# Weight loads and stores of the preparation issued from GpSimd's queue instead of SyncE's, in a scan layer beside a ternary feed-forward layer

## The reference, cut to what matters

```python
# x: (8, 4096, 1024) float32, one sequence of 4096 tokens for each core
xn = layernorm(x)
g = xn @ Wg + bg;  v = xn @ Wv + bv;  d = xn @ Wd + bd          # 1024 x 1024 each
h = linear_scan(sigmoid(g) * tanh(v), 0.001 + 0.998 * sigmoid(d))  # along the tokens

def weight_quant(w):      # ternary: each weight becomes -1, 0 or 1, times one scale
    scale = 1 / clip(mean(abs(w)), 1e-5)
    return clip(round(w * scale), -1, 1) / scale
def act_quant(x):         # 8 bits, one scale for each token
    scale = 127 / clip(max(abs(x), axis=-1), 1e-5)
    return clip(round(x * scale), -128, 127) / scale
gate = silu(act_quant(xn) @ weight_quant(w_gate).T)             # 4096 x 1024 weights
up   = act_quant(xn) @ weight_quant(w_up).T
f    = act_quant(gate * up) @ weight_quant(w_down).T            # 1024 x 4096 weights
out  = x + h + f
```

## Time and profile before

| | us |
|---|---|
| median of 3 runs | 7203.07 (7193.94 to 7207.64) |
| the profiled execution | 7188.56 |
| its span on the slowest core (core 6) | 7186.2 |
| spans of the eight cores | 7149.2 to 7186.2 |

### The profile page before, as it was taken

One profiled execution on the slowest core, in us unless ns is written; L12 is line 12 of the kernel. 1 busy time (PEld: TensorE's weight loads), 2 busy tenths in 40 slices (PEclk: granted clock), 3 DMA queues, 4 the chain that ended last, 5 costly groups with the idle time before them and its releaser, 6 DMA issues.

```text
span 7186.2 us, 44247 instructions; the slowest of 8 cores (7149.2 to 7186.2 us)
## 1 busy us (share of the span) xinstructions
PE 2267.5 (32%) x9490; PEld 1072.3 (15%) x9490; DVE 2914.1 (41%) x4898; ACT 396.1 (6%) x676; POOL 448.0 (6%) x481
## 2 busy tenths in 40 slices
PE   0022021021111021211010365555555555555553
PEld 0021011011110011111010122222222222222210
DVE  2344323325423333433332364445455455454441
ACT  1000000000000000000000000000000000000000
POOL 0000000000000000000000011111111111111111
PEclk9966555555555555555555687777777777777776
DMA  3122111122211111311111323333333333333334
GB/s 85 59 89 65 53 43 50 54 65 85 65 54 40 56 54 41 119 51 39 55 55 51 126 76 89 88 92 88 92 90 92 93 90 82 92 87 89 93 85 121
DMA packets 685093, 538.10 MB, mean 75 GB/s; under 512 B 532208, under 2 KB 532240, under 8 KB 682784
## 3 DMA queue, kind: packets, MB, share of 16 engines
q1 hardware_dynamic: 661760, 461.78, 23.0%
q0 software_dynamic: 23072, 73.50, 3.4%
HBM read 356.60 MB, written 109.05 MB: 65 GB/s over the span
## 4 chain that ended last, share of the span: by engine, by line
SPq 31%; DVE 29%; DMA 19%; PE 10%; issue 7%; ACT 2%; DVEq 1%; POOL 1%; ACTq 0%; POOLq 0%
SPq L423 13%; SPq L291 13%; DMA pqs<-scr_pqF 4%; PE pb L883 3%; PE pb L887 3%; PE pb L793 2%; DMA pbuf<-wdown 2%; SPq L579 2%; DMA pbuf<-wup 2%; DVE sg_slab L465 2%; DVE pqstage L468 2%; DMA pbuf<-wgate 2%; DMA qcm<-scr_acc 2%; DVE dvecs L376 2%; DVE x_grp L259 2%
## 5 line engine op out<-in xcount | busy, mean ns | idle before, releaser
L793 PE MATMUL pb<-wdr,pqs 128*128 128x512 bf16 x2048 | 651.0, 452 | 1367.8 <-DMA pqs<-scr_pqF 1043.0
L627 PE MATMUL pb<-wqu,wqg 128*128 128x256 bf16 x3072 | 493.9, 337 | 1742.4 <-DMA wqu<-scr_xn 1742.4
L883 PE MATMUL pb<-wqg,xqF_t 128*128 128x512 bf16 x2048 | 909.6, 444 | 325.6 <-DMA xqF_t<-scr_xqT 286.4
L887 PE MATMUL pb<-wqu,xqF_t 128*128 128x512 bf16 x2048 | 892.8, 436 | 0.0
L627 PEld LDWEIGHTS pb<-wqu,wqg 128*128 128x128 bf16 x3072 | 367.5, 121 | 1849.0 <-issue 1746.5
L907 DVE SCALAR_TENSOR_TENSOR pbuf<-pb,dvecs,epi 128x512 f32<-128x512 f32 x256 | 192.1, 751 | 1002.3 <-ACT epi L897 993.5
L595 PE MATMUL pb<-idf_sb,epi 128*128 128x128 f32 x256 | 81.3, 389 | 1423.6 <-DVE carry L652 1423.4
L253 POOL TENSOR_TENSOR qnd<-x_grp,qt 128x512 f32<-128x512 f32 x128 | 165.9, 1296 | 5001.2 <-DVE x_grp L250 5001.0
L793 PEld LDWEIGHTS pb<-wdr,pqs 128*128 128x128 bf16 x2048 | 200.6, 107 | 1727.7 <-issue 1590.9
L461 DVE TENSOR_SCALAR qt<-pbuf,wsc 128x512 f32<-128x512 f32 x111 | 54.0, 486 | 746.8 <-DMA pbuf<-wup 313.0
L645 DVE TENSOR_TENSOR epi<-epi 128x256 f32<-128x256 f32 x128 | 54.4, 425 | 706.1 <-ACT epi L642 694.5
(11 more groups left out here) (102 smaller groups left out, 2404.2 us busy)
## 6 DMA issues: line engine op xcount, KB each, us to landing
wdr<-scr_wdT SPq DMA_DIRECT2D x512, 256.0 KB, 3.0
pbuf<-wdown SPq DMA_DIRECT2D x64, 512.0 KB, 4.3
pbuf<-wgate SPq DMA_DIRECT2D x64, 512.0 KB, 4.1
pbuf<-wup SPq DMA_DIRECT2D x64, 512.0 KB, 3.7
scr_pqF<-pqstage POOLq DMA_DIRECT2D x64, 512.0 KB, 4.1
pqs<-scr_pqF SPq DMA_DIRECT2D x1024, 32.0 KB, 2.6
pbuf<-x SPq DMA_DIRECT2D x32, 512.0 KB, 3.5
x_grp<-x SPq DMA_DIRECT2D x32, 512.0 KB, 4.9
```

Of the source, the lines that this page charges most:

```text
L627: e.matmul(o, l, r, start=st, stop=sp),
L793: e.matmul(o, l, r, start=st, stop=sp),
L883: e.matmul(o, l, r, start=st, stop=sp),
L887: e.matmul(o, l, r, start=st, stop=sp),
```

## The change

The loads of the preparation (p_load, 192 of them) and its stores (p_store_cb, 96) are moved from the list of SP ("y") to that of POOL ("g"). The loads get four semaphores of their own (PL0 to PL3); before, they shared LP0 to LP3 with loads of stage 3. The waits on both stay as they were, and so do their places among the instructions of the program as a whole; only the list differs in which they stand. The transposes stay on SP. After the line for the new names and the one for the list PL, line numbers are one higher up to p_store_cb and beyond (L359 becomes L360, L423 becomes L424, L437 becomes L438).

```diff
--- before.py
+++ after.py
@@ -150,7 +150,7 @@
                  "TD0", "TD1", "TD2", "TD3", "TD4", "TD5", "TD6", "TD7", "SN", "WT",
                  "SW1", "SW2", "SW3", "GC",
                  "SA", "SX", "SW", "SP", "SP2", "SO0", "SO1", "SXT0", "SXT1",
-                 "PD0", "PD1", "PD2", "PD3"]
+                 "PD0", "PD1", "PD2", "PD3", "PL0", "PL1", "PL2", "PL3"]
         sems = {n: SemC(n) for n in names}
         for smc in sems.values():
             smc.h = es.enter_context(nc.semaphore(smc.name))
@@ -165,6 +165,7 @@
         SP2 = sems["SP2"]
         SXT = [sems["SXT0"], sems["SXT1"]]
         PD = [sems[f"PD{j}"] for j in range(4)]
+        PL = [sems[f"PL{j}"] for j in range(4)]
         SO = [sems["SO0"], sems["SO1"]]
         TD = [sems[f"TD{j}"] for j in range(8)]
         SN, WT = sems["SN"], sems["WT"]
@@ -356,9 +357,9 @@
                 g = (wv(V), wv(S))
             else:
                 g = (g,)
-            op("y", lambda e, o=wchunk[slot], i_=src_ap: e.dma_start(out=o, in_=i_),
-               sem=LP[slot], inc=16, wait=g)
-            return slot, wv(LP[slot])
+            op("g", lambda e, o=wchunk[slot], i_=src_ap: e.dma_start(out=o, in_=i_),
+               sem=PL[slot], inc=16, wait=g)
+            return slot, wv(PL[slot])
 
         runpair = {"d": (scal[:, 4:5], scal[:, 5:6]),
                    "g": (scal[:, 6:7], scal[:, 7:8]),
@@ -432,7 +433,7 @@
         def p_store_cb(li, gmarks, gdst, mat):
             g8 = li // 8
             for j in range(8):
-                op("y", lambda e, i_=xbig[:, j * 1024:(j + 1) * 1024],
+                op("g", lambda e, i_=xbig[:, j * 1024:(j + 1) * 1024],
                    o=gdst(g8, j):
                    e.dma_start(out=o, in_=i_), sem=SWs[j % 4], inc=16,
                    wait=gmarks if j == 0 else ())
```

## The result

The changed kernel took 6343.35 us in the median of 8 runs (6337.12 to 6353.39), against 7197.94 for the kernel before beside it (8 runs, 7190.82 to 7219.04). The ratio is 0.8811, with a 95% interval of 0.8800 to 0.8822: 855 us less. 6310 was forecast, with a range of 6235 to 6440, and 893 us less. So the time lies in the range, and the saving is 38 us smaller than the sum.

What follows compares the result with a forecast made beforehand. The bound was the order of SP's list, each load behind eight transposes. Even groups 295, odd 341, mixed 153, tail 80, stage 3 4, mean items 20: 893 us saved, 7203 - 893 = 6310 us, range 6235 to 6440.

Steps and rivals of the forecast that it cites:

- rival of issue time alone: Only SP's issue time for loads and stores is saved, 165 us, so 7040 us; chance 0.03.
- A set at 10.1 us: Stage 2: eight transposes on SP take 10.1 us per chunk, and SP decides the pace.
- the tail: Last ten sets, where only the preparation runs: 191.8 us become 111.6 with one stall, 80 saved.
- The stall at 10.6 us: After each eighth chunk SP stands still 10.6 us for the stores wherever another set of transposes follows at once.
- cost nothing more: Loads behind the stores in POOL's list go out 4 to 5 us after SP stopped, there when the stores are.
- The four mixed groups: Groups 5, 7, 11 and 13: 15 distances between sets fall from 20.9 to 10.1 us, less 10: 153 saved.
- Full groups: Quant-only groups: even 183.3 us with stall, 295 saved; odd 184.7, or 174.1 without stall, 341 saved.
- Mean items: Step 4 of five groups: DVE no longer idles 4.04 us for a load behind scr_acc stores; 20 us saved.
- Into stage 3: Weight loads begin 5.9 us earlier but share the engines with 2 MB of stores: 4 us saved.
- The rule on POOL's descriptors: Skill's warning that POOL's DMAs wait during DVE's two-port operations; would cost 36 us more, saving 857.
- Rival 1: Transposes beside loads: sets of 11.0 us and stalls of 14, 117 us less saved, 6430 us; chance 0.12.
- Rivals 3 and 4: Third: stall hidden, mean items gain more, 6215 us, chance 0.05. Fourth: POOL's list becomes the chain, 7270 us, 0.02.

Runs made afterwards that it cites:

- e3: Kernel before, all DMAs still on SP, each chunk's load put into SP's list ahead of the transposes owed for the chunk before: 0.8889, 6403 us.
- e2: Changed kernel with the preparation's loads back on SP, only its stores on POOL: 0.9976, 7186 us.
- e5: Changed kernel with two buffers xbig in turn, so transposes wait for the stores of the set before the last: 0.8811, 6347 us.
- e4: Changed kernel with the preparation's loads on ACT's list instead of POOL's, stores still on POOL: 0.8742, 6297 us.
- e7: Changed kernel, each chunk's load moving only 32 of 1024 columns, all waits and issues kept: 0.8728, 6287 us.
- e15: Changed kernel with two buffers xbig, loads and scr_acc stores on ACT's list, next group's x load issued in step 4: 0.8532, 6146 us.

## Why the prediction was right

**What bounds the kernel.** Shown. e3 takes the load out from behind the transposes and changes nothing else, and 800 us go. The rival of issue time alone (7040) is refuted by e2 and e3 together. The Trainium skill's sentence under "Issuing engines are not separate DMA queues" ("DMA: Bandwidth & Descriptors") says that issuing from several engines saves only the sequencer's time for an issue. The change saved 855 us, where the issue time moved off SP is 165. The 800 us that e3 gains on SP alone are no issue time but the wait in the list. In the 56 us between e3 and the change issue time is one part (192 loads of about 0.52 us are 100 us, not all on the path); against it the change loses 17 us to e3 from the x loads to the xn stores (584.6 against 567.8), so its worth isn't separated. No run here tests what the page says of bandwidth.

**A set at 10.1 us, the tail.** Ten sets with one stall took 113.1 us, 111.6 were forecast. Without the stall of 11.3 that is 10.2 for a set. SP decides there, as said.

**The stall at 10.6 us.** 11.4 in group 3, and 11.5 in the mean of eight (10.8 to 11.8). The sum has these eight; the nine in the rivals, and in what I expected of e5, are one too many, since of the 12 sets of stores three have no further set of their matrix behind them and one stands at the end of group 2. The price was about right, but its worth was not a free term: e5 takes it away and gains nothing, since the loads behind the stores come just as late. The sentence that these loads "cost nothing more" is right for full groups with one buffer. It fails in groups 5 and 11, where no set of transposes follows and DVE's mean items wait in the stall's place; I had put 10 us there for both together with another extra, and e4 gains 36 in them. This did not show in the sum, because another thing that I hadn't counted cancels it: before, DVE waited in the same two groups just as long for mean loads behind SP's list, 23.3 and 21.9 us, and in the change it waits 24.0 and 21.8. The four mixed groups saved 157 us, 153 were forecast, and that this term came out so close is luck.

**Full groups.** The even ones took 191.1, 189.6, 186.8 and 185.6 us (forecast 183.3), the odd ones 191.9, 192.6, 183.8 and, without a stall, 179.0 (forecast 184.7 and 174.1). Saved: 275 and 323 us instead of 295 and 341 (the differences of the prediction add up to 342 for the odd ones, 1 us more than it says). This term was mis-sized by 38 us. With e7's small loads the same eight groups take 1475 us, against 1500 in the change, so 26 of the 38 go with the bytes of the loads. 12 of these lie in the seven stalls, which are 9.8 us long in e7 in the mean; with no big loads beside them, eight stores have all landed 8.0 us after the first one's issue, with them after about 9.8. Of the other 12 about 5 are sets of 10.2 us instead of 10.1, and the rest isn't taken apart.

**Mean items.** Forecast 20 us saved, four of them in a mixed group; the four mean groups saved 9. DVE's waits for mean loads fell in them from 44 to 30 us, but from the x load to the xn stores they took 8 us longer, 4.4 of them in group 1.

**Into stage 3.** Forecast 4 us, measured 2 over stages 2 to 3 together. In order of time, as in the earlier trace rows:

```profile
3152.07 4.99 SPq L681 DMA_DIRECT2D wqg<-scr_wgT  x8
3153.40 4.27 POOL L438 DMA_DIRECT2D scr_wuT<-wqu  x8 [53.14 <-DMA wqu<-pqstage]
3177.32 3.71 SPq L686 DMA_DIRECT2D wqu<-scr_wuT  x8
```

SP's first weight loads do begin right behind the last transposes. But they are ahead of the stores now: L686 waits for those until 3177.32, 24 us after POOL began to issue them, where before it was under 12. From the first weight load to the end the kernel took 3192 us, 4 more than before.

Together: 275 + 323 + 157 + 79 + 9 + 2 = 845 us, against 842.2 between the two spans. So by the traces 48 us of the sum's 893 are missing, 38 in the full groups and 11 in the mean items, with -4, 1 and 2 in the other terms. The medians are 855 us apart, since the profiled execution before lay 9 us under the median and that of the change 3 us above it.

**The rule on POOL's descriptors** (the Trainium skill, "SBUF — State Buffer", the "DVE blocks DMA" trap). Issues of loads beside DVE's operations took 527 ns in the median and 725 at most, of stores 539 and 552. A starved load would also land late. In the change, with the loads on POOL's list:

```profile
pbuf<-wdown POOLq DMA_DIRECT2D x64, 512.0 KB, 5.3
pbuf<-wgate POOLq DMA_DIRECT2D x64, 512.0 KB, 4.8
pbuf<-wup POOLq DMA_DIRECT2D x64, 512.0 KB, 4.6
```

In e4, with the same loads on ACT's list:

```profile
pbuf<-wdown ACTq DMA_DIRECT2D x64, 512.0 KB, 5.2
pbuf<-wgate ACTq DMA_DIRECT2D x64, 512.0 KB, 4.4
pbuf<-wup ACTq DMA_DIRECT2D x64, 512.0 KB, 4.6
```

The medians differ by 0.4 us at most, so no run shows starving of a size that counts here. A small cost of POOL's own is not excluded (the 18 and 29 us above).

**The rivals.** Rival 1 (sets and stalls longer beside loads) is right for the stalls, 11.5 us against 9.8 in e7, and not for the sets, which take 10.2 in the change and in e7 alike. In its own terms it comes to 14 us (96 sets, eight stalls) and not 117. Rivals 3 and 4 didn't come.

## What to carry to other kernels

Look at what stands ahead of a load in its engine's list before asking for a faster load or a deeper buffer: four buffers were there all along, and they were of no use as long as each load stood behind eight transposes. Moving the load one place up did nearly as much as giving it another engine. On the new engine the same thing comes back: there stores that wait held the loads, and a second buffer was worth nothing until they were kept apart (0.8811 with both on one list, 0.8674 apart, 0.8699 on one list with the stores placed later).

## What the runs showed that I had not expected

- Loads that run ahead aren't free. With POOL up to four chunks ahead, the x loads' median landing went from 4.9 to 5.9 us, and 20 us were lost at the groups' beginnings; ACT's list, which holds each load until its step, had 5.0. It matters only where x is waited for: in e15, which loads x early, x takes 5.9 us in the median as well, and it is the fastest version.
- The last 2 MB of stores, whose issue began 1.3 us after that of 8 MB of loads on another engine, took 8.7 to 20.0 us to land, where 4.1 is the median of that line. Before, the same stores were issued ahead of these loads and landed in 3.7 to 5.8 us.
- ACT took 192 loads and 64 stores into its list besides its activations, and the fastest version is one that does so (e15).
